# The causal convolution of v, moved from ScalarE and GpSimd to VectorE's padded buffer

## What is computed

```python
q = _l2norm(einsum('bsd,de->bse', hidden_states, Wq).reshape(b, s, H, D))
k = _l2norm(einsum('bsd,de->bse', hidden_states, Wk).reshape(b, s, H, D))
v = einsum('bsd,de->bse', hidden_states, Wv).reshape(b, s, H, D)
# depthwise causal convolution over the sequence, K = 4 taps, then silu
q = _causal_dwconv_silu(q, conv_q)
k = _causal_dwconv_silu(k, conv_k)
v = _causal_dwconv_silu(v, conv_v)
```

## Time and profile before

| what | value |
|---|---|
| device time, median of 3 runs | 1710.4 us |
| the three runs | 1701.67, 1710.4, 1733.17 us |
| span of the profiled execution | 1705.8 us |
| what the page shows of that execution outside its span | nothing |
| instructions | 25,673 |
| mean granted clock of TensorE | 0.919 |

### The profile page before, as it was taken

One profiled execution on the slowest core, in us unless ns is written; L12 is line 12 of the kernel. 1 busy time (PEld: TensorE's weight loads), 2 busy tenths in 40 slices (PEclk: granted clock), 3 DMA queues, 4 the chain that ended last, 5 costly groups with the idle time before them and its releaser, 6 DMA issues.

```text
span 1705.8 us, 25673 instructions
## 1 busy us (share of the span) xinstructions
PE 1461.6 (86%) x9434; PEld 1185.9 (70%) x9434; DVE 1112.7 (65%) x2013; ACT 560.4 (33%) x1082; POOL 392.1 (23%) x351
## 2 busy tenths in 40 slices
PE   5786899999878699999978699999978599999977
PEld 4432788888733588888833488888853378888866
DVE  4399576667469567667549756766729856666742
ACT  1286222222268322122148422212228522222221
POOL 5034022212124112112124211221214311211210
PEclk8798899899999799899989799989989789999986
DMA  4000100000000010000000010000000000000001
GB/s 107 1 0 1 50 1 1 0 0 0 1 14 1 3 48 1 0 0 0 1 14 1 0 50 1 0 0 0 0 15 0 1 1 1 1 0 0 0 1 25
DMA packets 12493, 14.59 MB, mean 9 GB/s; under 512 B 3124, under 2 KB 8310, under 8 KB 12406
## 3 DMA queue, kind: packets, MB, share of 16 engines
q1 hardware_dynamic: 12406, 13.48, 2.7%
HBM read 12.43 MB, written 1.05 MB: 8 GB/s over the span
## 4 chain that ended last, share of the span: by engine, by line
PE 52%; DVE 25%; issue 19%; ACT 2%; POOL 1%; SPq 1%; DVEq 1%; POOLq 0%; DMA 0%; ACTq 0%
PE bank L653 9%; PE bank L707 8%; PE bank L703 8%; PE bank L690 5%; DVE qkv L950 4%; DVE ks L983 4%; PE bank L821 4%; DVE kq L981 3%; DVE tot L984 2%; PE bank L667 2%; PE bank L723 2%; PE bank L659 2%; PE bank L714 2%; DVE nmat L989 2%; DVE aq L990 2%
## 5 line engine op out<-in xcount | busy, mean ns | idle before, releaser
L653 PE MATMUL bank<-kq,ks 128*128 128x128 f32 x1536 | 231.6, 296 | 53.1 <-DVE tot L984 47.2
L981 DVE TENSOR_TENSOR kq<-kq,tot 128x512 f32<-128x512 f32 x160 | 138.4, 865 | 194.5 <-PE bank L653 191.4
L653 PEld LDWEIGHTS bank<-kq,ks 128*128 128x128 f32 x1536 | 200.9, 202 | 69.2 <-DVE tot L984 59.9
L629 PE MATMUL bank<-hT,gw 128*128 128x512 f32 x384 | 185.7, 621 | 38.1 <-DVE region L957 19.1
L950 DVE SCALAR_TENSOR_TENSOR qkv<-region,gchan,qkv 128x512 f32<-128x512 f32 x192 | 201.1, 1099 | 0.0
L371 POOL TENSOR_TENSOR qkv<-qkv,kq 128x509 f32<-128x509 f32 (+2 forms) x96 | 133.2, 1388 | 282.9 <-ACT qkv L454 277.9
L690 PE MATMUL bank<-region,nmat 128*128 128x64 f32 x1280 | 173.4, 280 | 2.3
L707 PE MATMUL bank<-tt,fmat 128*128 128x64 f32 x1280 | 170.6, 277 | 5.5 <-DVE fmat L1019 5.5
L629 PEld LDWEIGHTS bank<-hT,gw 128*128 128x128 f32 x384 | 73.6, 198 | 142.7 <-issue 103.7
L690 PEld LDWEIGHTS bank<-region,nmat 128*128 128x128 f32 x1280 | 163.6, 199 | 12.4 <-DVE nmat L989 7.5
L707 PEld LDWEIGHTS bank<-tt,fmat 128*128 128x128 f32 x1280 | 160.6, 195 | 7.5 <-DVE fmat L1019 6.0
(11 more groups left out here) (156 smaller groups left out, 2419.6 us busy)
## 6 DMA issues: line engine op xcount, KB each, us to landing
gw<-in_L_attn_Wq SPq DMA_DIRECT2D x4, 512.0 KB, 4.0
gw<-in_L_attn_Wk SPq DMA_DIRECT2D x4, 512.0 KB, 5.0
gw<-in_L_attn_Wv SPq DMA_DIRECT2D x4, 512.0 KB, 6.0
gwo<-in_L_attn_Wo SPq DMA_DIRECT2D x4, 512.0 KB, 4.9
x<-in_L_attn_hidden_states SPq DMA_DIRECT2D x2, 512.0 KB, 6.1
gfb<-in_L_attn_Wfb SPq DMA_DIRECT2D x4, 256.0 KB, 6.2
ggb<-in_L_attn_Wgb SPq DMA_DIRECT2D x4, 256.0 KB, 7.3
out<-x SPq DMA_DIRECT2D x2, 512.0 KB, 5.5
```

Of the source, the lines that this page charges most:

```text
L629: last = eng.matmul(bank[t][:, :], gw[:, t, kt, cols], hT[:, kt, toks], start=(kt == 0), stop=(kt == KT - 1))
L653: last = eng.matmul(o[:, :, u, :].rearrange("p a (n t) -> p a n t", t=h), unit(ks[:, p], u), half(kq[:, p, :, u * P:(u + 1) * P], h, 1), s ...
L981: eng.tensor_tensor(half(kq[:, p], h, 1), half(kq[:, p], h, 1), lower.rearrange("p (a n o) -> p a n o", a=1, o=1).broadcast_to((P, 2, nb, ...
```

## The change

The padded buffer gets a third row. ScalarE copies v unscaled from PSUM into it, once the convolutions of the item before are done (`conved`), and VectorE convolves three rows rather than two, after a wait for that copy. ScalarE's scaled copies, `vtap`, GpSimd's loop over items and the semaphore `v_chain` go; the counts of `conv_chain` and `conved` go from two to three per step. With three rows `pad` reaches nine elements into part 9 of `region`, `es`, which is written after the stage.

```diff
-        pad = region[:, 6 * UN:6 * UN + 2 * PADW].rearrange("p (a s) -> p a s", a=2)
+        pad = region[:, 6 * UN:6 * UN + 3 * PADW].rearrange("p (a s) -> p a s", a=3)
...
-        vtap = [kq[:, 0, 0], kq[:, 0, 1], kq[:, 1, 0]]
...
@@ gpsimd, in the loop over groups @@
-                for hh in range(G):
-                    for b in range(B):
-                        i = g * ITEMS + hh * B + b
-                        eng.wait_ge(v_taps, i + 1)
-                        for tap in range(TAPS - 1):
-                            shift = TAPS - 1 - tap
-                            o = qkv[:, 2, hh, b, shift:]
-                            if tap:
-                                eng.wait_ge(v_chain, (TAPS - 1) * i + tap)
-                            eng.tensor_tensor(o, o, vtap[tap][:, 0:S - shift], ALU.add).then_inc(v_chain, 1)
                 head(g * NCH, 0)
@@ scalar, item @@
                 if j:
-                    eng.wait_ge(v_chain, (TAPS - 1) * i)
-                for tap in range(TAPS):
-                    o = vtap[tap] if tap < TAPS - 1 else qkv[:, 2, hh, b, :]
-                    last = eng.activation(o, bank[2][:, :], ACT.Copy, scale=gchan[:, 2 * TAPS + tap, hh:hh + 1])
-                last.then_inc(v_taps, 1)
+                    eng.wait_ge(conved, 3 * i)
+                eng.activation(pad[:, 2, TAPS - 1:], bank[2][:, :], ACT.Copy).then_inc(v_taps, 1)
@@ scalar, before the first head @@
-                eng.wait_ge(conved, 2 * ITEMS * g + 2 * ITEMS)
-                eng.wait_ge(v_chain, (TAPS - 1) * ITEMS * g + (TAPS - 1) * ITEMS)
+                eng.wait_ge(conved, 3 * ITEMS * g + 3 * ITEMS)
@@ vector, item @@
-                chained = 2 * (TAPS - 1)
+                chained = 3 * (TAPS - 1)
...
                 def conv(tap):
-                    for t in range(2):
+                    for t in range(3):
...
-                            eng.wait_ge(conv_chain, chained * i + 2 * (tap - 1) + t + 1)
+                            eng.wait_ge(conv_chain, chained * i + 3 * (tap - 1) + t + 1)
...
                 for t in range(2):
                     if j:
-                        eng.wait_ge(conved, 2 * i - 1 + t)
+                        eng.wait_ge(conved, 3 * i - 2 + t)
...
                 eng.wait_ge(normed, 2 * i + 2)
+                eng.wait_ge(v_taps, i + 1)
                 conv(0)
```

More of the change, by code:

```diff
@@ L171, in build @@
             "sq_ready z_ready z_exp z_ln sp_ready dec_ready")
-        n_ln, r_ready, normed, conv_chain, conved, v_taps, v_chain, gate_done, gated = sems(
-            "n_ln r_ready normed conv_chain conved v_taps v_chain gate_done gated")
+        n_ln, r_ready, normed, conv_chain, conved, v_taps, gate_done, gated = sems(
+            "n_ln r_ready normed conv_chain conved v_taps gate_done gated")
         kb_ready, es_ready, ks_ready, qs_ready, vs_ready, qk_ready, kq_ready = sems(
```

## The result

The changed kernel takes 1753.1 us in the median (four runs, 1748.0 to 1779.4) against 1709.9 (1701.7 to 1733.2): a ratio of 1.026, 95% interval 1.022 to 1.030. I had said 1714.6 and 1695 to 1734. Medians here are over all runs of a kernel; the ratios and their intervals leave out runs of more than 1.5% over its fastest. The profiled execution of the changed kernel took 1749.4 us, its span is 1747.6, 41.8 over the 1705.8 of before.

What follows compares the result with a forecast made beforehand. VectorE's issue was taken to bound each item. Per group -0.30 + 1.35 + 0 = +1.05 us, four groups +4.2, took the span from 1705.8 to 1710.0; 4.6 more for the median gave 1714.6 us, range 1695 to 1734.

Steps and rivals of the forecast that it cites:

- an item costs what VectorE issues: Item stage: VectorE's instructions follow one another without waiting, 9.49 us per item before, 9.78 us forecast after.
- The 2.09 us taken off taps 1 and 2: Per item on VectorE: without GpSimd's adds beside them, four tap instructions take 2.64 us instead of 4.73.
- the 2.38 us added: Per item on VectorE: four new instructions for the third row, one of 0.40 us and three of 0.66.
- the price of 0.66 and 0.40 us an instruction: VectorE's convolution: 0.66 us per later tap, read from tap 3 with GpSimd silent, and 0.40 per tap 0.
- the copy of v in time: ScalarE's copy between items: round trip 0.85 us against 1.31 of VectorE's work, 0.46 to spare; late-copy rival 0.03.
- the last tap hidden under the table load: End of each group's last item: the added tap ends 0.08 us before ScalarE's table load does, costing nothing.
- GpSimd's adds were the cause of the slow taps: Taps 1 and 2 of an item: about 2.0 of 9.49 us; the rival that GpSimd is innocent had 0.02.
- the 213 us for L950: Sign in the profile: 288 later-tap instructions at about 0.74 us mean, 213 us in all, against 201.1 before.
- the sum per group: Item stage of a group: -0.30 for item 1, +1.35 for the following items, 0 at the end: +1.05 us.
- The new wait costs nothing or 0.1: Item 1: VectorE's wait for ScalarE's copy of v before tap 0, put at nothing or 0.1 us.
- The clock: Rival, scan: clock falls come or go, 4.9 us each, one per group, 20 us: 1695 or 1734; chance 0.22.
- the same view shows one slot of 39.2 us in each of the four groups now, so it may well stay so: Scan: the argument against the shifted-clock rival, that the slow slots may stay as they are.

Runs made afterwards that it cites:

- b_noadd: b_f1 without GpSimd's three adds per item, so v is convolved with one tap; its one run took 1652.8 us.
- a_pool: a_f1 with GpSimd's three adds per item put back on spare buffers, computing nothing that is used; its one run took 1791.0 us.
- a_f1w: a_f1 with VectorE's wait for ScalarE's copy of v moved two instructions later, to just ahead of tap 0 of v; 1700.5 us.
- a_f1: The changed kernel with one extra 128x256 float32 TensorE product per scan slot, in the hole ahead of the third inverse; 1710.2 us.
- b_f1: The kernel before with one extra 128x256 float32 TensorE product per scan slot, in the hole ahead of the third inverse; 1693.1 us.
- a_f3: The changed kernel with three such extra TensorE products per scan slot, two of them without a hole; 1752.8 us.
- b_f3: The kernel before with three such extra TensorE products per scan slot, two of them without a hole; 1746.6 us.
- b_d1: The kernel before with one extra VectorE instruction of 0.66 us ahead of each group's last item; ratio 1.033.
- b_d5: The kernel before with five extra VectorE instructions, 3.3 us a group, ahead of each group's last item; ratio 0.998.

## Why the prediction was wrong

What held: an item costs what VectorE issues. The 2.09 us taken off taps 1 and 2, the 2.38 us added, the price of 0.66 and 0.40 us an instruction, the copy of v in time, the last tap hidden under the table load: the profile has them to 0.03 us. That GpSimd's adds were the cause of the slow taps is shown by b_noadd, where the taps take 0.66 us each without them; a_pool shows that adds put back slow whichever instruction of VectorE they meet, there tap 0. One sign was misread: the 213 us for L950 is a sum of durations, the 201.1 of the page counts overlaps once. The mean of 744 ns came as forecast, and the page's figure for it is 195.9 us. So the balance is real: VectorE wins back nearly as much as it takes on.

What was mis-sized: the sum per group, +1.05 us predicted, +1.88 measured. The step was "The new wait costs nothing or 0.1": I took it as nothing in items 2 to 8. It costs 0.09 in each of the eight, as a second semaphore wait right behind the one for the products; moved by two instructions it costs nothing (a_f1w). 8 x 0.09 is 0.7 of the 0.83 us that are missing.

What failed, and put the time outside the range: the forecast took the scan over as it was. The clock was among the rivals, with 4.9 us a fall, at most one fall a group either way, 20 us in all and a chance of 0.22. The price of a fall was read from the one kind of slow slot that the kernel before has. Even that was too low, as the slot behind the one of 39.18 us takes 35.49, 1.2 over the common one. Its worst kind isn't in that trace: 44 us, 9.9 over a common slot, followed by up to four more slots over the common one, 34 us in one group. The trace did hold a warning that I read as comfort, "the same view shows one slot of 39.2 us in each of the four groups now, so it may well stay so". Three distances of 395.8 to 395.9 us say that this kernel repeats its groups, not that another one would: even here the slow slot is the third in two groups and the fourth in the other two. The delays show it: of three delays in the kernel before, from 0.66 to 3.3 us a group, two cost 59 and 72 us in the median, 47 and 38 by their fastest runs. The range should have reached to 1780 at least. The rival was the right one, but at one fall of 4.9 us a group it could not give 1753.

How much of the 43 us is the change's? Of the span's 41.8, 7.5 are in its item stages, 28.8 in the slots of the scan and 5.5 around them. The part in the slots follows the clock: with the one product it is 959.6 us in the changed kernel (a_f1) and 951.0 in the kernel before (b_f1), in place of 999.7 and 970.9. With one more product per slot in both kernels the difference is 17 us (a_f1, b_f1), with three it is 6 (a_f3, b_f3), and of the 17 some 9 are still slow slots of a_f1. 7.5 us, 0.4%, is what the change costs in its own stage; the rest is where it happened to put the scan.

The Trainium skill's page "TensorE: Matmul & The Clock Gate", section "What's actually happening", says that for modelling the ramp is under 1% of a typical kernel's span. It says so of the warm-up when a kernel starts, which no run here sets apart, and it can't be carried over to falls in the middle of a kernel: between b_d1 and b_d5, the same program but for four instructions a group, lie 3.6%, and the slots of the scan take 1014.2 us in the one and 953.2 in the other.

The formula of the Trainium skill's page "VectorE: DVE Perf Modes", section on the TRN2 errata, which I had set aside, gives 0.59 and 0.33 us for VectorE's instructions. It stays aside: they take 0.66 and 0.40 from start to start here, in nine taps as in two.

What stays open: what it is in a slot that the clock reacts to. The falls began 19.7 to 19.9 us into the slots of 44 us, behind some 15 us of products of 64 and 128 columns, and one product of 256 columns there kept the slots of 44 us off and most of the others; but three products left more. No experiment took the columns and the idle time apart. Nor was it tried whether the 0.6 us hole alone is to blame. The hole and the products are there in the slots without a fall as well, as the two windows of the kernel before show.

## What to carry to other kernels

When a stage's length changes, ask what the next stage does if it begins a microsecond later: look at the granted clock there, and if it falls even once in a stage that is bound by TensorE, count the whole stage at risk, in both directions. Before believing that an edit cost or gained 2 to 4% in such a kernel, put the same delay, and another one, into the kernel without the edit. And price an engine's instructions from rows in which its neighbour is silent: GpSimd's adds looked free beside a VectorE that never idled, and were 2 us of every 9.5.

## What the runs showed of the hardware

- 0.66 us of VectorE's work ahead of each scan made the kernel 3.3% slower (b_d1), 3.3 us of it made no difference (b_d5, 0.998). In the slots of 44 us the granted clock fell from 1.00 to 0.50 after 20 us in which TensorE was busy 87 to 91% and had no idle gap of over 1.7 us (changed kernel, b_d1).
- While GpSimd does a two-input add on SBUF, VectorE's `tensor_scalar` on SBUF stands too: three took 3.31 to 3.97 us against 1.19 (a_pool), 2.1 to 2.8 us lost beside three adds, where the two-input taps lost 2.09. The Trainium skill's page "SBUF — State Buffer", section "SBUF: two separate sides", has it so: an exclusive lock, for VectorE's two-port modes as for two SBUF inputs. The trace of a_pool agrees: each of the three instructions ends 0.28 us behind one of the adds (at 117.33, 118.57 and 119.97 us, the adds at 117.05, 118.28 and 119.69).
- Two semaphore waits in a row on VectorE, the first of them for the instruction just ahead, cost 0.09 us more than with the second moved two instructions on: (79.87 - 79.15) / 8 (a_f1, a_f1w).
